# Last feed-forward of a four-layer gated cross-attention block: GpSimd adds and subtracts the rounding's magic numbers, with two batches in flight

## What is computed

```python
x = x + jnp.tanh(g_xattn[3]) * _L3_xattn_ref(_layernorm(x), ctx_4096, ...)
x = x + jnp.tanh(g_ffn[3]) * _L3_ffn_ref(_layernorm(x), w_gate, w_up, w_down)

def _L3_ffn_ref(x, w_gate, w_up, w_down):      # 512 -> 1376 -> 512
    gate = _mx_linear(x, w_gate)
    up = _mx_linear(x, w_up)
    return _mx_linear(jax.nn.silu(gate) * up, w_down)

def _mx_linear(x, w):                          # activations to 3 mantissa bits, weights to 1
    return jnp.matmul(_mx_quant(x, 3), _mx_quant(w, 1).T)

def _mx_quant(x, mbits):                       # blocks of 32 along the columns
    amax = jnp.max(jnp.abs(xb), axis=-1, keepdims=True)
    scale = jnp.exp2(jnp.floor(jnp.log2(amax)) - 2)
    e = jnp.maximum(jnp.floor(jnp.log2(jnp.abs(xb / scale))), 0.0)
    q = jnp.round(xb / scale / jnp.exp2(e - mbits)) * jnp.exp2(e - mbits)
    return jnp.clip(q, -max_norm, max_norm) * scale
```

## Time and profile before

| | us |
|---|---|
| median of 3 runs (lowest to highest) | 1731.21 (1729.58 to 1731.86) |
| profiled execution | 1732.03 |
| its span | 1730.3 |
| busy in it: PE, DVE, ACT, POOL | 1442.4, 1014.9, 355.4, 69.4 |
| last feed-forward, from its first transpose to the end | 1564.2 to 1730.3 |
| busy there: PE, DVE, ACT, POOL | 83.76, 110.97, 30.79, 0.00 |

### The profile page before, as it was taken

How to read it: one execution, slowest core, us unless ns; L and a number is a source line. 1 busy time by engine, 2 the same in 40 slices (tenths; PEclk the granted TensorE clock), 3 DMA queues, 4 the chain that set the end, 5 groups by cost and what they waited for, 6 DMA issues and landing times. The chain is left out here.

```text
span 1730.3 us, 26582 instructions
## 1 busy us (share of the span) xinstructions
PE 1442.4 (83%) x8867; PEld 897.2 (52%) x8875; DVE 1014.9 (59%) x1651; ACT 355.4 (21%) x705; POOL 69.4 (4%) x101
## 2 busy tenths in 40 slices
PE   0799957999999966997999999999796799985553
PEld 0566723444444435665677777775444566532221
DVE  2677558788772136232566666677243457777665
ACT  0333221111113012101121212121101233222121
POOL 3000011000000000000000000000013000000000
PEclk9899858999999988898999999998697899998776
DMA  5000010111000037000000000000400000000000
GB/s 202 1 0 0 1 37 19 37 37 36 18 14 1 0 95 167 0 0 11 22 21 18 24 20 25 25 25 15 104 0 1 1 1 1 0 1 6 12 12 19
DMA packets 52312, 44.56 MB, mean 26 GB/s; under 512 B 38498, under 2 KB 38690, under 8 KB 51363
## 3 DMA queue, kind: packets, MB, share of 16 engines
q1 hardware_dynamic: 52258, 43.85, 8.5%
HBM read 41.74 MB, written 2.10 MB: 25 GB/s over the span
## 5 line engine op out<-in xcount | busy, mean ns | idle before, releaser
L924 DVE TENSOR_SCALAR f_side<-f_chunk 128x1536 f16<-128x1536 f32 x165 | 148.1, 953 | 45.5 <-PE f_sum L768 44.2
L768 PE MATMUL f_sum<-f_side,f_diag 128*128 128x512 f16 x495 | 122.4, 390 | 8.6 <-DVE f_side L924 7.2
L768 PEld LDWEIGHTS f_sum<-f_side,f_diag 128*128 128x128 f16 x495 | 48.1, 100 | 90.8 <-issue 45.0
L1565 PE MATMUL a_ps_b<-h_all,weights_a 128*128 (+1 forms) x768 | 92.1, 279 | 1.3 <-PEq L124 1.3
L1565 PEld LDWEIGHTS a_ps_b<-h_all,weights_a 128*128 128x128 f32 x768 | 89.1, 195 | 5.9 <-issue 5.9
L1653 PE MATMUL a_ps_y<-weights_a,a_o_t 128*128 128x512 f32 x192 | 89.3, 612 | 2.7 <-DVE a_v_ones L1785 2.0
L787 PE MATMUL f_gate<-h_all,f_w_t 128*128 128x512 f32 (+1 forms) x176 | 86.7, 593 | 0.0
L787 PE MATMUL f_up<-h_all,f_w_t 128*128 128x512 f32 (+1 forms) x176 | 79.6, 592 | 0.0
L839 PE MATMUL f_sum<-weights_a 128*128 128x512 f32 (+1 forms) x176 | 75.7, 592 | 0.0
L446 PE MATMUL a_o<-weights_a 128*128 128x128 f32 x512 | 71.7, 292 | 0.0
L382 PE MATMUL a_proj<-h_all,a_wqk 128*128 (+1 forms) x64 | 36.8, 687 | 40.7 <-PEq L375 39.4
(11 more groups left out here) (334 smaller groups left out, 2698.7 us busy)
## 6 DMA issues: line engine op xcount, KB each, us to landing
f_chunk<-in_l_w SPq DMA_DIRECT2D x30, 256.0 KB, 3.0
weights_a<-in_l_wgu SPq DMA_DIRECT2D x16, 232.0 KB
weights_a<-in_l_wq SPq DMA_DIRECT2D x48, 64.0 KB, 2.4
weights_a<-in_l_wo SPq DMA_DIRECT2D x1, 3072.0 KB, 11.7
weights_a<-in_l_wd SPq DMA_DIRECT2D x16, 192.0 KB, 3.1
x_res<-in_x SPq DMA_DIRECT2D x1, 2048.0 KB, 8.2
ctx_nat<-in_ctx SPq DMA_DIRECT2D x1, 2048.0 KB, 13.5
ctx_tr<-in_ctx_tr SPq DMA_DIRECT2D x4, 512.0 KB, 13.5
```

The costliest lines, as they stand in the source:

```text
L768: mm = nc.tensor.matmul(psum[:, j, :], diag[:, k, :], side[:, k % RING, j * D:(j + 1) * D], start=(k == 0), stop=(k == LEVELS - 1), skip_g ...
L924: nc.vector.tensor_scalar(side[:, k % RING, :], wch[:, u, :], bounds[k], steps[k][0], ALU.is_le if k < ZERO else ALU.is_gt, ALU.mult).then ...
L1565: mm = nc.tensor.matmul(pb[:, u % 2, g * P:(g + 1) * P], wq_of(k, u, g), h_t[:, k, bass.ds(b * P, P)], start=(k == 0), stop=(k == KT - 1))
```

## The change

`gate`, `up` and `silu` get three banks or slices, one for each chunk, and `ptr` shrinks from two banks to one, used in turn by the input's transposes and by the two halves of the hidden transposes. `hid`, the rounder's buffers and the new `shifted` exist twice. GpSimd gets a loop with hid + m (in place) and that minus m into `shifted`; m is written over the exponents. DVE's rounding is split: `begun` holds products, powers, scales and m; `ended` holds the clip, which waits for GpSimd. PE's step becomes hidden transposes and down of b, then input transposes and gate and up of b+2.

```diff
-        mh = MxRounder(nc, HF, lambda n, w, d: sb("mx_hid_" + n, [P, w], d), lambda n: sem("mx_hid_" + n))
+        mh = [MxRounder(nc, HF, lambda n, w, d: sb(f"mx_hid{u}_" + n, [P, w], d)[:, :], lambda n: sem(f"mx_hid{u}_" + n),
+                        in_place=True) for u in range(2)]
-        sil = sb("silu", [P, 2, D])
-        hid = sb("hidden", [P, HF])
+        sil = sb("silu", [P, 3, D])
+        hid = sb("hidden", [P, 2, HF])
+        shifted = sb("hidden_shifted", [P, 2, HF], BF16)
-        ptr = ps("tr", [P, 2, 2 * D], BF16)
-        pg, pu, pd = ps("gate", [P, 2, D]), ps("up", [P, 2, D]), ps("down", [P, D])
+        ptr = ps("tr", [P, 2 * D], BF16)
+        pg, pu, pd = ps("gate", [P, 3, D]), ps("up", [P, 3, D]), ps("down", [P, D])
...
+            @block.gpsimd
+            def _(pool):
+                with pool.Fori(0, NB // 2) as pair:
+                    for u in range(2):
+                        m = mh[u].ma[0:P, 0:HF]
+                        after(pool, mh[u].s_ma, pair + 1)
+                        nc.gpsimd.tensor_tensor(hid[:, u, :], hid[:, u, :], m, ALU.add).then_inc(mh[u].s_t1, 1)
+                        after(pool, mh[u].s_t1, pair * 3 + 1)
+                        nc.gpsimd.tensor_tensor(shifted[:, u, :], hid[:, u, :], m, ALU.subtract).then_inc(mh[u].s_t1, 1)
...
                 def hidden_transposed(b):
                     after(pe, s_hq, b + 1)
                     for half in range(2):
+                        if half:
+                            after(pe, s_ht, b * 3 + 5)
...
                 def step(b):
-                    x_transposed(b + 1)
-                    gate_and_up(b + 1, 0)
-                    gate_and_up(b + 1, 1)
                     hidden_transposed(b)
-                    gate_and_up(b + 1, 2)
                     down(b)
+                    x_transposed(b + 2)
+                    gate_and_up(b + 2)
...
+                def begun(pair, u):
+                    b = pair * 2 + u
+                    products(b, u)
+                    after(dve, s_hid, b * 3 + 3)
+                    mh[u].powers(dve, hid[:, u, :], P, HF)
+                    mh[u].scales(dve, pair, P, HF, 3)
+                    mh[u].magic(dve, pair, P, HF, 3)
+
+                def ended(pair, u):
+                    mh[u].clip(dve, pair, hq[:, :], P, HF, s_hq, t2=shifted[:, u, :])
...
-                products(0, range(3))
-                hidden_rounded(0)
-                with dve.Fori(1, NB) as b:
-                    products(b, range(3))
-                    updated(b - 1)
-                    hidden_rounded(b)
+                begun(0, 0)
+                begun(0, 1)
+                ended(0, 0)
+                with dve.Fori(1, NB // 2) as pair:
+                    begun(pair, 0)
+                    updated(pair * 2 - 2)
+                    ended(pair - 1, 1)
+                    begun(pair, 1)
+                    updated(pair * 2 - 1)
+                    ended(pair, 0)
+                updated(NB - 2)
+                ended(NB // 2 - 1, 1)
                 updated(NB - 1)
```

More of the change, by code:

```diff
@@ L2593, in _, with x_transposed @@
                 sp.wait_ge(chip.s_out, 16 * NB)
+            @block.gpsimd
[7 more added lines that the diff above has]
+                        nc.gpsimd.tensor_tensor(shifted[:, u, :], hid[:, u, :], m, ALU.subtract).then_inc(mh[u].s_t1, 1)
             @block.tensor
             def _(pe):
-                def x_transposed(b):
+                def x_transposed(b, first=False):
+                    if not first:
+                        after(pe, s_ht, b * 3 - 2)
                     for k in range(KT):
-                        mm = nc.tensor.transpose(ptr[:, 0, k * P:(k + 1) * P], rounded.of(b)[:, k * P:(k + 1) * P],
+                        mm = nc.tensor.transpose(ptr[:, k * P:(k + 1) * P], rounded.of(b)[:, k * P:(k + 1) * P],
                                                  chip.ident16[:])
@@ L2602, in x_transposed, with gate_and_up @@
                     after(pe, s_xt, b + 1)
[L2604 to L2619, removed]
+                def gate_and_up(b, first=False):
+                    for n, (at, c) in enumerate(CH):
+                        if not first:
+                            after(pe, s_hid, b * 3 + (n - 2))
+                        for k in range(KT):
+                            mm = nc.tensor.matmul(pg[:, n, 0:c], xt[:, k, :], wg[:, k, at:at + c],
+                                                  start=(k == 0), stop=(k == KT - 1))
+                        mm.then_inc(s_g, 1)
+                        for k in range(KT):
+                            mm = nc.tensor.matmul(pu[:, n, 0:c], xt[:, k, :], wu[:, k, at:at + c],
+                                                  start=(k == 0), stop=(k == KT - 1))
+                        mm.then_inc(s_u, 1)
                 def hidden_transposed(b):
@@ L2635, in down @@
                     mm.then_inc(s_y, 1)
[L2637 to L2640, removed]
                 def step(b):
-                    x_transposed(b + 1)
-                    gate_and_up(b + 1, 0)
-                    gate_and_up(b + 1, 1)
                     hidden_transposed(b)
-                    gate_and_up(b + 1, 2)
                     down(b)
+                    x_transposed(b + 2)
+                    gate_and_up(b + 2)
+                pe.sem_inc(s_ht, 4)
+                x_transposed(0, first=True)
+                gate_and_up(0, first=True)
+                x_transposed(1, first=True)
+                gate_and_up(1)
+                pe.wait_ge(rounded.s_xq, 1)
                 with pe.Fori(0, NB - 2) as b:
                     step(b)
-                pe.wait_ge(rounded.s_xq, 1)
-                step(NB - 2)
+                hidden_transposed(NB - 2)
+                down(NB - 2)
                 hidden_transposed(NB - 1)
@@ L2660, in x_stored @@
                     after(act, s_xp, b + 1)
[L2661 to L2668, removed]
+                    nc.scalar.copy(xt[:, :, :], ptr[:, 0:D].rearrange("p (k t) -> p k t", k=KT)).then_inc(s_xt, 1)
@@ L2670, in hidden_stored, with silu @@
+                def silu(b):
+                    for n, (at, c) in enumerate(CH):
+                        after(act, s_g, b * 3 + (n + 1))
+                        nc.scalar.activation(sil[:, n, 0:c], pg[:, n, 0:c], ACT.Silu).then_inc(s_sil, 1)
                 def hidden_stored(b):
                     after(act, s_hp, b * 2 + 1)
-                    nc.scalar.copy(ht[:, 0:8, :], ptr[:, 0, :].rearrange("p (m t) -> p m t", m=8)).then_inc(s_ht, 1)
+                    nc.scalar.copy(ht[:, 0:8, :], ptr[:, :].rearrange("p (m t) -> p m t", m=8)).then_inc(s_ht, 1)
@@ L2678, in _ @@
                 x_stored(0)
[L2679 to L2685, removed]
+                silu(0)
+                x_stored(1)
+                silu(1)
+                with act.Fori(0, NB - 2) as b:
                     hidden_stored(b)
-                    silu(b + 1, 2)
+                    x_stored(b + 2)
+                    silu(b + 2)
```

19 lines of the change are left out of this document (8 added, 11 removed).

## The result

| | before | after |
|---|---|---|
| median | 1731.53 us (1729.58 to 1733.35) | 1790.64 us (1789.72 to 1794.23) |
| ratio | | 1.0345, 95% interval 1.0327 to 1.0364 |
| profiled execution | 1732.03 us | 1790.98 us, span 1789.3 us |
| one turn of the last stage | 18.6 to 19.9 us, mean 19.3 | 28.6 to 29.7 us, mean 29.3 |

What follows compares the result with a forecast made beforehand. No engine is full; a chain from engine to engine bounds the last feed-forward. From first transposes at 1591.1, six turns of 24.1 + 2.3 = 26.4 us reach 1749.5, the tail 1774.3; forecast 1775 us, range 1748 to 1806.

Steps and rivals of the forecast that it cites:

- The ring: Last feed-forward: batches in flight never overlap, a turn is DVE's part plus PE's part, 24.1 us against 18.6 to 19.9 before.
- transposes to down: PE, start of the hidden transposes to the start of the down projection: 2.57 us plus 0.75 for the single bank, 3.32.
- down: PE's down projection, 11 matmuls: 2.17 us at the full clock or 4.87 as in the last batch; 4.7 taken.
- input transposes to the gate: PE, from the input transposes to the first gate matmul: 1.5 us a turn.
- gate to exponents: First gate matmul to DVE's exponents, through gate, up and the last product: 5.4 us, or 10.0 at the 1.2 GHz level.
- exponents to the end of m: DVE's rounding from the exponents until m is written: 5.0 us a turn.
- clip, with what GpSimd adds: DVE's clip until PE's hidden transposes: 3.47 us, plus 2.26 us a turn for GpSimd's passes running beside it.
- GpSimd beside the clip: GpSimd's add and subtract slow DVE's two clip passes: 2.26 us a turn taken, with ends of 0 and 5.95.
- a stretch: Main case: DVE's clip passes lengthen 1.71 times beside GpSimd's passes, 2.26 us a turn; 1765 to 1790 us, chance 0.45.
- full wait: Rival: DVE's clip passes wait out GpSimd's add and subtract, 5.95 us a turn; turns of 30.1, 1801 us, chance 0.25.
- No stretch: Rival: DVE's clip costs what it did despite GpSimd; turns of 24.1, 1758 us, chance 0.20.
- Open ring: Rival: PE does gate and up of b+2 while DVE works on b+1; turns of 11.2, 1681 us, chance 0.04.

Runs made afterwards that it cites:

- e1: The changed kernel, with GpSimd's add of batch n also waiting until the clip of batch n-1 is written; 1754.4 us, 1.0145 of the kernel before.
- e6: The changed kernel with GpSimd's add and subtract each cut into four instructions of 352, 352, 352 and 320 columns; 1768.8 us, 1.0214 of before.
- e3: The changed kernel with PE's input transposes and gate and up of b+2 ahead of the hidden transposes and down of b; 1714.7 us, 0.9887 of before.

## Why the prediction was right, and where it was off

**The ring was right in its sum.** The prediction's terms against the turn at 1619.34:

| term | forecast, us | after, us |
|---|---|---|
| transposes to down | 3.32 | 3.95 |
| down | 4.7 | 4.27 |
| input transposes to the gate | 1.5 | 1.64 |
| gate to exponents | 5.4 | 5.74 |
| exponents to the end of m | 5.0 | 4.78 |
| update | 0.75 | 0.66 |
| clip, with what GpSimd adds | 3.47 + 2.26 | 8.66 |

The first two rows belong together: the trace shows ten of down's eleven matmuls here, but its first weight load at 1622.88; with a matmul of 0.43 us there the two are 3.5 and 4.7. The terms ahead of the clip are then off by up to 0.35, in both directions. The mean turn of 29.3 less the 5.2 us of waiting is 24.1, the forecast sum; e1, in which no clip pass waits, measures 23.9. DVE's idle time ahead of the products (12.15 us), GpSimd's passes right behind m with nobody waiting for their end in the loop (e1), and down at about 430 ns a matmul are as forecast; PE's idle time ahead of the transposes, forecast as about the same, is 15.04, longer by what the clip lost. So were the levels of the clock: the granted clock is 0.50 (1.2 GHz) from 1619.34 to 1627.56 and 1.00 (2.4 GHz) in the gates, 1629.20 to 1634.00. That the turn is 29.3 and not 26.4 us is the work of the last row.

**The mis-sized term is GpSimd beside the clip.** It was taken as 2.26 us a turn, by the ratio 1.71 of the small operations in the earlier trace rows, with ends of 0 and 5.95. It measured 2.55 + 2.65 = 5.2. Six turns of 2.9 more, 17.5 us, and a first batch 1.3 later (transposes 28.1 behind the stage's start, not 26.85), less a tail 1.3 shorter (23.5 from the transposes of batch 6 to the end, not 24.8) and a stage that started 2.5 earlier, give the 15.0 us by which the span missed 1774.3.

So the case to which 0.45 was given, a stretch, did not happen. The rival "full wait" did, at its own price: the pass of 3.08 us (estimated as 3.3) and a turn of 29.3 in place of 30.1 put it at 1791 in place of 1801. The time lies in the range because the range took in this rival; the sum itself was 15.6 us short. The step that failed is the reading of the earlier trace rows as a rate, 1.71 times, that carries over to an operation some nine times as long (1.59 us against 0.168). What sets the delay is how long the other engine's instruction still has to run: cut into pieces, the same passes delay the clip by 0.4 and 0.5 us (e6). Taken one by one, the rows behind the earlier trace rows held a sign of it:

```profile
1298.60 0.92 POOL L2057 TENSOR_SCALAR weights_a<-f_raw_queries,weights_a 128x256 f32<-128x256 f32 x1
...
1299.01 0.54 DVE L1996 TENSOR_SCALAR f_combine<-f_iota_f,f_index_f,f_top 128x8 f32<-128x8 f32 x1
```

The longest L1996 ends at 1299.55, 0.03 us behind the GpSimd instruction, and the next longest (1301.79, 0.46 us) 0.03 behind another (1301.29, 0.93 us), just as a wait for its end would have it. But the two L1999 beside GpSimd took 0.29 us and ended inside a GpSimd instruction. Why they lost only 0.12 us was not tried and stays open, and with it whether every GpSimd operation shuts DVE out as these adds and subtracts do.

The Trainium skill, page "SBUF — State Buffer", section "Who interferes with whom", says what was then measured: the one that starts first keeps the port pair for its whole instruction, and the other blocks. The traces of the clip agree in both directions. In the turn above the clip waited for the add; in the first batch the clip pass started 0.26 us ahead, and it was the add that took 4.26:

```profile
1583.81 1.58 DVE L1431 TENSOR_TENSOR f_hidden_shifted<-f_hidden_shifted,f_mx_hid_limit 128x1376 bf16<-128x1376 bf16 x1
...
1584.07 4.26 POOL L2603 TENSOR_TENSOR f_hidden<-f_hidden,f_mx_hid_exponents 128x1376 f32<-128x1376 f32 x1 [2.02 <-DVE f_mx_hid_exponents L1413]
```

**The rivals.** "No stretch" (1758) is what e1 builds, at 1754. "Open ring" was priced at 1681 on the ground that DVE would set the pace at 11.2 us a turn; e3 shows that moving the gates alone leaves a second ring through the update (15.8), and only with the passes out of the way as well is the turn 11.4 to 13.1, by the clock that PE is granted.

## What to carry to other kernels

Two batches in flight need an order in which, on every in-order engine, no operation of the next batch stands behind one that waits for this batch: two pairs of lines changed places on PE (and ACT's copies with them), and the same kernel went from 3.4% slower to 1.1% faster. Work given to GpSimd is only beside DVE's if the DVE operations that it meets are not those that it shuts out: look at which ones run at that time, and if they must meet, let the longer side wait by a semaphore, or cut it into pieces. A DVE instruction that is longer than its usual time is the sign; it shows as busy time, not as a wait.

## What was not expected of the hardware

The prediction priced the exclusion for the clip alone. It takes in operations with one input from SBUF too, and small ones. These are rows of after while the first batch's passes run on GpSimd:

```profile
1575.29 3.09 POOL L2603 TENSOR_TENSOR f_hidden<-f_hidden,f_mx_hid_exponents 128x1376 f32<-128x1376 f32 x1 [14.94 <-DVE f_mx_hid_exponents L1413]
...
1576.76 2.35 DVE L1392 TENSOR_SCALAR f_mx_hid_exponents<-f_hidden 128x1376 uint32<-128x1376 uint32 x1
...
1578.56 3.48 POOL L2605 TENSOR_TENSOR f_hidden_shifted<-f_hidden,f_mx_hid_exponents 128x1376 bf16<-128x1376 f32 x1 [0.19 <-POOL f_hidden L2603]
...
1579.14 1.59 DVE L1401 TENSOR_REDUCE f_mx_hid_largest_power<-f_mx_hid_exponents 128x43 f32<-128x1376 f32 x1
...
1580.76 1.33 DVE L1404 TENSOR_SCALAR f_mx_hid_limit<-f_mx_hid_largest_power 128x43 bf16<-128x43 f32 x1
```

The exponents take 2.35 us (0.88 alone) and end 0.73 behind the add; an operation on 43 columns, 0.19 us alone, takes 1.33 and ends 0.05 behind the subtract. The reduction between them, with the subtract running beside it, keeps its 1.59 us. The Trainium skill, in the same section of the page "SBUF — State Buffer", says that an operation on a tensor and a scalar (`tensor_scalar`, as both of these are) can enter a two-port mode and then contends too, and that a reduction never does on this chip. The rows agree with both, though in which mode the two operations ran no trace here shows.
